# Attention on TensorE: two units' transposes and then two units' scores, in place of one and one

## What is computed

```python
sim = jnp.einsum('bhid,bjd->bhij', q, k)          # j runs over 1 + 512 keys
sim = sim + bias                                  # bias: one 512 x 512 table per head, and a null column
sim = jnp.where(causal_mask, neg, sim)
sim = jnp.where(mask_p[:, None, None, :], sim, neg)
attn = jax.nn.softmax(sim, axis=-1)
out = jnp.einsum('bhij,bjd->bhid', attn, v)
out = out.transpose(0, 2, 1, 3).reshape(b, n, INNER)
out = out @ Wo
return layernorm(out, g_out)
```

## Time and profile before

| | |
|---|---|
| median of 3 runs | 1794.83 us (1790.31 to 1797.67) |
| profiled execution | 1795.32 us, span 1793.6 us |
| TensorE matmuls busy | 1631.7 us, 91% of the span |
| VectorE, ScalarE, GpSimd busy | 54%, 40%, 41% |
| mean granted TensorE clock | 0.967 |

### The profile page before, as it was taken

One profiled execution on the slowest core, in us unless ns is written; L12 is line 12 of the kernel. 1 busy time (PEld: TensorE's weight loads), 2 busy tenths in 40 slices (PEclk: granted clock), 3 DMA queues, 4 the chain that ended last, 5 costly groups with the idle time before them and its releaser, 6 DMA issues. The chain is left out here.

```text
span 1793.6 us, 36160 instructions
## 1 busy us (share of the span) xinstructions
PE 1631.7 (91%) x10364; PEld 1362.8 (76%) x10365; DVE 974.2 (54%) x2442; ACT 714.9 (40%) x1823; POOL 730.2 (41%) x1177
## 2 busy tenths in 40 slices
PE   6899996999999999996988987989999999999998
PEld 4677775888888888885777776777777788778886
DVE  5444525776676676775554554653333333356555
ACT  3222324776676676774222121213333343321221
POOL 1000234675576676674554553142222222134222
PEclk9999998999999999998999998989999999989999
DMA  6566657776776766775444344015446633246333
GB/s 214 192 224 203 225 209 211 214 218 181 210 209 183 214 199 181 212 215 148 147 134 136 128 134 153 0 55 203 176 147 268 217 108 108 88 119 216 111 100 112
DMA packets 172361, 301.32 MB, mean 168 GB/s; under 512 B 16658, under 2 KB 64322, under 8 KB 170196
## 3 DMA queue, kind: packets, MB, share of 16 engines
q1 hardware_dynamic: 142324, 235.21, 41.1%
q0 software_dynamic: 11200, 35.73, 6.9%
q10 hardware_dynamic: 18720, 29.12, 4.7%
HBM read 186.99 MB, written 113.00 MB: 167 GB/s over the span
## 5 line engine op out<-in xcount | busy, mean ns | idle before, releaser
L754 POOL TENSOR_SCALAR probs<-probs,rsums 128x512 f32<-128x512 f32 (+3 forms) x512 | 264.0, 532 | 203.8 <-DVE rsums L790 203.4
L782 DVE CUSTOM_DVE_ANT_0 scores<-psum,resident 128x514 f32<-128x514 f32 (+3 forms) x512 | 243.2, 484 | 158.8 <-PE psum L897 136.9
L855 ACT ACTIVATE probs<-scores,lowest 128x514 f32<-128x514 f32 (+3 forms) x512 | 284.2, 557 | 34.1 <-DVE lowest L782 33.1
L909 PE MATMUL psum<-ident,probs 128*128 128x128 f32 x1280 | 235.1, 283 | 21.3 <-DVE probsT L797 14.0
L897 PE MATMUL psum<-keys,queries 128*128 (+4 forms) x640 | 222.6, 356 | 23.8 <-DMA queries_and_ones<-q_hi_d 17.8
L909 PEld LDWEIGHTS psum<-ident,probs 128*128 128x128 f32 x1280 | 152.3, 142 | 54.4 <-issue 39.5
L897 PE MATMUL psum<-keys_lo_and_mask,queries_and_ones 128*128 (+4 forms) x640 | 185.2, 298 | 0.0
L929 PE MATMUL psum<-probsT,v_now 128*64 128x128 f32 x2560 | 168.3, 278 | 0.9 <-DVE probsT L797 0.9
L897 PEld LDWEIGHTS psum<-keys,queries 128*128 128x128 f32 x640 | 127.7, 199 | 35.0 <-issue 21.0
L864 ACT ACTIVATE probsT<-psum 128x512 f32<-128x512 f32 (+2 forms) x192 | 93.6, 487 | 137.7 <-PE psum L909 120.2
L929 PEld LDWEIGHTS psum<-probsT,v_now 128*64 128x64 f32 x2560 | 137.4, 137 | 14.4 <-issue 1.6
(11 more groups left out here) (240 smaller groups left out, 3696.1 us busy)
## 6 DMA issues: line engine op xcount, KB each, us to landing
ys_d<-y_out ACTq DMA_DIRECT2D x71, 256.0 KB, 2.0
q_hi_d<-q_hi SPq DMA_DIRECT2D x64, 256.0 KB, 2.5
q_lo_d<-q_lo SPq DMA_DIRECT2D x64, 256.0 KB, 2.9
queries<-q_hi_d SPq DMA_DIRECT2D x64, 256.0 KB, 3.7
queries<-q_lo_d SPq DMA_DIRECT2D x64, 256.0 KB, 4.2
queries_and_ones<-q_hi_d SPq DMA_DIRECT2D x64, 256.0 KB, 4.5
oT_d<-o_out SPq DMA_DIRECT2D x64, 256.0 KB, 2.2
o_in<-oT_d SPq DMA_DIRECT2D x32, 512.0 KB, 3.9
```

Of the source, the lines that this page charges most:

```text
L754: pool.tensor_scalar(out=row, in0=row, scalar1=rsums[:, n % RING:n % RING + 1], scalar2=1.0, op0=ALU.mult, op1=ALU.mult).then_inc(probs_sc ...
L782: dve.tensor_tensor_reduce(out=scores[n % 4][:, 0:CK[i]], in0=score_psum(n), in1=bias_of(resident, i, h), scale=1.0, scalar=3.0e38, op0=AL ...
L855: act.activation(probs[n % RING][:, 0:CK[i]], scores[n % 4][:, 0:CK[i]], ACT.Exp, bias=lowest[:, n % 4:n % 4 + 1], scale=-1.0, accum_out=s ...
L909: last = pe.transpose(probsT_bank[g % 2][:, at + j * P:at + (j + 1) * P], probs[n % RING][:, AHEAD + j * P:AHEAD + (j + 1) * P], ident[:])
```

## The change

TensorE's `body` takes the units two by two: first the transposes of both, then the scores of the two units that are 10 ahead. `weigh_values` comes behind the second and the sixth unit of a head pair, as before. No other engine's program is edited.

```diff
             def body(b, first=False, last=False):
-                for n in range(UB):
-                    transpose_probs(b, n)
-                    if n + LEAD < UB:
-                        score(b, n + LEAD)
-                    elif not last:
-                        score(b + 1, n + LEAD - UB)
-                    if n % QUAD == 1:
+
+                for n in range(0, UB, 2):
+                    for u in (n, n + 1):
+                        transpose_probs(b, u)
+                    for u in (n, n + 1):
+                        if u + LEAD < UB:
+                            score(b, u + LEAD)
+                        elif not last:
+                            score(b + 1, u + LEAD - UB)
+                    if n % QUAD == 0:
                         g = n // QUAD - 1
                         if g >= 0:
                             weigh_values(b, g)
```

## The result

The changed kernel takes 1820.51 us at the median of 4 runs (1816.38 to 1825.02); the kernel before, with one more run, 1796.25. The ratio is 1.0136 with a 95% interval of 1.0094 to 1.0178: 24 us slower, where 1819 us was forecast.

The account below looks back on a forecast made before the run. It took a TensorE-VectorE cycle of 8.03 us per head pair as the bound, growing to 8.47. 21.6 + 1.3 + 1.1 = 24.0 us on the profiled 1795.3 gave 1819.3, forecast 1819 us against the run median; range 1807 to 1830.

Parts of the forecast that it names:

- The cycle: Per head pair: 6.07 us TensorE work from T1 (unit 1's transpose) to S0 (wide scores), 1.96 us VectorE bias and copy.
- The two moves: Unit 7's transpose goes ahead of the wide scores, unit 2's scores behind unit 1's transpose; each adds 0.22 us a period.
- Rival (c): VectorE's copy doesn't hold unit 1's transpose, or other slack hides the longer path: no change, 1795 us; chance 0.08.
- Alternating: Switching between transposes and scores on TensorE was costed at 0, bound 0.03 us for each of eight alternations removed.
- rival (b): Alternating has a price TensorE saves: gain to 1773 us (chance 0.05) or smaller loss, 1807 us (chance 0.05).
- T6's thin cover: Unit 6's transpose waits for VectorE's copy of unit 4's bank; slack falls from 0.16 to 0.05 us, costed at nothing.
- rival (a): Cover lost at unit 6's transpose: a second stop of about 0.1 us a period, 1825 us; chance 0.13.
- rival (d): Repeated 0.75 us TensorE stops lower its clock for two units of each period: 63 us more, 1882 us; chance 0.03.
- GpSimd's cover: GpSimd's scaling of probabilities is done units ahead of TensorE's transposes; TensorE waited twice; cover said to hold, nothing priced.
- The six periods with a wait for queries: Periods where the wide scores also wait for a DMA, 3.2 us in all; 0.22 us each counted, 1.3 us together.
- The five turns of the loop: Periods where engines' loops go round and TensorE waits for VectorE's bias; 0.22 us each, 1.1 us together.
- 49 ordinary periods: Head pairs where unit 1's transpose waits only for VectorE's copy; 0.44 us more each, 21.6 us together.

## Why the prediction was right, and where it was not

**The cycle.** The step that mattered was to close the cycle, 6.07 + 1.96 = 8.03, instead of reading TensorE's 91% or its 0.25 us stops. The new period of 8.47 us came out to the hundredth, the stop of 0.76 (0.75 forecast) within one. The two moves at 0.22 us each are confirmed one at a time, and what holds T1 is confirmed by taking the copy out from behind the bias. Rival (c) is out.

**Alternating.** Costed at nothing, bound 0.03 us: in the middle groups, with no stop left on TensorE, 7.51 against 7.52. In the changed kernel itself the work from T1 to S0 grew by 0.44 us (6.07 to 6.51), which leaves the alternations on that path nothing, so rival (b) is out as an account of this result. Beside the narrow scores of units 0 and 1 the price wasn't taken by itself: there, with units 0 and 1 apart and the copy first, S2 took 0.05 us more than I had counted.

**T6's thin cover.** The copy of T4's bank ends at 606.85 in the changed kernel (606.32 + 0.53), and T6 starts at 607.06: with the 0.15 us that lie between such a copy and a transpose, 0.06 us are left, where 0.05 was forecast. No wait stands there; rival (a) didn't come, but a slip of one more narrow transpose would have brought it.

**The clock.** The two windows of the changed kernel: a stretch in the middle, and the whole stage.

```profile
core 0: us, PE busy (x) PEld busy (x) DVE busy (x) ACT busy (x) POOL busy (x), PEclk, DMA share, GB/s
500.00:531.00 31.00, 25.85 (x257) 22.24 (x255) 20.00 (x72) 19.88 (x63) 19.46 (x37) 1.00 0.60 171
282.00:854.00 572.00, 505.86 (x5120) 447.04 (x5120) 387.59 (x1408) 392.54 (x1216) 360.67 (x664) 0.99 0.66 192
```

Stops of 0.76 us in every period leave the granted clock at 1.00, so rival (d) is out for stops of this length. The Trainium skill's rule (TensorE: Matmul & The Clock Gate, "A second HAM failure mode: psum-queue depth-cycling") isn't borne out here.

**GpSimd's cover: the step that failed.** I put this term at nothing ("Nothing there is priced"). In an ordinary pair that holds; at the turn of a sequence it doesn't. TensorE at the first pair of a sequence in the changed kernel:

```profile
366.86 0.44 PE L909 MATMUL psum<-ident,probs 128*128 128x128 f32 x2
367.55 0.44 PE L909 MATMUL psum<-ident,probs 128*128 128x128 f32 x2 [0.25 <-POOL probs L754]
```

and GpSimd there:

```profile
363.57 0.40 POOL L763 COPY v_now<-values 128x256 f32 x1 [1.12 <-PE psum L929]
363.94 1.04 POOL L754 TENSOR_SCALAR probs<-probs,rsums 128x384 f32<-128x384 f32 x2
364.94 0.18 POOL L742 TENSOR_TENSOR spare_pool<-ident 1x1 f32<-1x1 f32 x1
365.07 0.60 POOL L744 CAST w_hi<-w_in 128x512 fp32r<-128x512 f32 x1
365.75 1.28 POOL L746 TENSOR_TENSOR w_lo<-w_in,w_hi 128x512 fp32r<-128x512 f32 x1
367.01 2.16 POOL L754 TENSOR_SCALAR probs<-probs,rsums 128x256 f32<-128x256 f32 x4
```

T7 is asked for a whole wide unit's scores (some 0.5 us) earlier than before, and its probabilities are scaled only behind the copy of the values and the split of a weight tile, which GpSimd does in between, the first once a sequence, the second in six pairs of eight. TensorE's stops for GpSimd grew from 1.9 to 4.6 us, and a stop costs more than its bracket: T7 stands 0.69 us behind T6 here (366.86 to 367.55), 0.28 in an ordinary pair, so the 0.25 shown are 0.41. Apart from one stop of 1.49 us at the stage's start, which both kernels have, the changed kernel has ten of them, all in the first pair of a sequence: five at T7, and five of 0.32 to 0.36 us at T5, which is now asked for right behind T4. I had looked at an ordinary pair, where the scaling is well ahead, and not at the one where GpSimd has the most else to do.

**The few special periods.** One reading of mine was wrong here, and one count. The six periods with a wait for queries took 53.3 us in both kernels, where I had counted 6 x 0.22 = 1.3 us more. I had read the load as issued just before the S0 that waits for it; it is issued a whole head pair ahead (behind S7 of the pair before the last). So it gained not only T7's 0.22 us but the longer period too: from the last matmul of such an S7 to the S0 in question it was, by the ordinary pair of TensorE's timelines, 8.03 + 1.65 = 9.68 us (606.57 - 604.92 = 1.65) and is 8.47 + 1.87 = 10.34 (607.47 - 605.60 = 1.87), 0.66 us more, and the waits gave back 1.9 us. The five turns of the loop took 57.9 before and 59.4 after, 1.6 us more where I had 1.1.

The count: 49 + 6 + 5 are 60 periods of the 62. The 55 of the table leaves out six T1, at first pairs of a sequence, that stood still for some 0.12 us, as at 355.32, behind a matmul that ends at 354.93 + 0.28 = 355.21; they too waited for the copy, and in the changed kernel 63 T1 wait, hence 47.6 us and not 41. The two periods that I left out took 2.0 us more, 0.9 for the cycle and most of the rest with the stops for GpSimd at the first pairs of sequences 1 and 7.

So the 25.5 us of the stage are, in the two profiled executions: 49 ordinary periods 21.7 (21.6 forecast), the six with a load 0.0 (1.3), the five turns 1.6 (1.1), the two left out 2.0 (none), and the last pair 0.2 (none). The large term was right by its mechanism. The small misses have both signs and partly cancel, and the medians are 24.3 us apart; that the sum of 24.0 us comes closer than its small terms is luck.

## What to carry to other kernels

Where a pipeline repeats, look for the cycle that closes to the measured period (the engine's own work from the resource it got to the work it hands over, plus the other engine's answer), and ask of each reordered instruction on which side of the hand-over it lies: work that leaves the waiting part costs its full length, even if no bracketed stop grows. Where shown lengths overlap, the bracket isn't the loss; measure from start to start. And before judging an order on one engine, look at the order of the engine that answers: here the same edit cost 24 us or, with one copy moved ahead, was part of a gain of 24.

## What the runs showed that was not expected

The bracketed stop before T1 was no measure of the loss: 0.25 us at a period of 8.25 us (units 0 and 1 apart) as at 8.03, with the 0.22 us standing unbracketed at S2. Two edits that each lose by themselves (1.0136 and 1.0071) gain together (0.9868). And TensorE can go through a head pair in 7.52 us (median) without a stop, with its own order and the place of one copy changed, where the kernel before looked 91% busy.
